# Graph attention kernel, edge stage: VectorE builds the two one-hot matrices of a chunk in four pieces each

## The reference

```python
def gt_layer(x, ntype, etype, src, dst, Wk, Wq, Wv, Wa, Watt, Wmsg, pri, skip, g, b):
    k = typed_linear(x, ntype, Wk).reshape(n, H, HS)        # q, v likewise; H = 8, HS = 16
    kT = jnp.einsum('nhd,htdo->nhto', k, Watt)              # one row per node and edge type
    vT = jnp.einsum('nhd,htdo->nhto', v, Wmsg)
    kw, m = kT[src, :, etype], vT[src, :, etype]
    a = jnp.einsum('ehd,ehd->eh', kw, q[dst]) * pri[:, etype].T / SQRT_D
    att = edge_softmax(a, dst, n)                           # softmax over the edges of one destination
    hag = jax.ops.segment_sum((m * att[:, :, None]).reshape(-1, H * HS), dst, num_segments=n)
    h = jax.nn.silu(typed_linear(hag, ntype, Wa))
    alpha = jax.nn.sigmoid(skip[ntype])[:, None]
    h = h * alpha + x * (1.0 - alpha)
    return layernorm(h) * g + b
# twice, then: layernorm(x + h @ ff_w + ff_b)
```

## Time and profile before

| what | value |
|---|---|
| device time, median of three executions | 8303.22 us |
| the profiled execution: span from first to last instruction | 7619.3 us |
| the rest of the median, outside the span | 683.9 us |
| busy POOL / DVE / PE / ACT in the span | 4322.7 / 3763.8 / 4483.6 / 1445.3 us |
| granted TensorE clock, mean over the span | 0.721 |
| L903, gathers issued by POOL | 3136 issues, 3453.7 us busy |
| L951, `to_rank` on DVE | 198 of 2283 ns |
| L946, `of_rank` on DVE | 200 of 1287 ns |

### The profile page before, as it was taken

The page is one execution under the profiler, slowest core; times in us unless marked ns, Lnnn a source line. Parts: engine busy times, 40 slices in busy tenths (PEclk is TensorE's granted clock), DMA queues, the critical chain, the costliest instruction groups (busy, mean ns, idle before and its releaser), DMA issues. The chain is left out here.

```text
span 7619.3 us, 79126 instructions
## 1 busy us (share of the span) xinstructions
PE 4483.6 (59%) x18423; PEld 3236.2 (42%) x18424; DVE 3763.8 (49%) x5261; ACT 1445.3 (19%) x3714; POOL 4322.7 (57%) x4007
## 2 busy tenths in 40 slices
PE   0128999566666665654318999566666665665221
PEld 0113443555555555554203444455555555555111
DVE  1224443555555555554374444455555555554473
ACT  0013333111111111112112333111111111111111
POOL 0543222777777777775303222677777777776305
PEclk9569999666766666666559999766666666676555
DMA  3125776666666666665103777666666666666101
GB/s 68 39 45 220 297 297 281 160 178 166 177 165 176 167 171 170 170 172 122 29 19 150 297 297 296 181 168 174 169 173 168 176 166 176 169 173 159 34 0 35
DMA packets 809561, 1228.51 MB, mean 161 GB/s; under 512 B 152983, under 2 KB 623978, under 8 KB 758833
## 3 DMA queue, kind: packets, MB, share of 16 engines
q0 software_dynamic: 223248, 853.51, 33.6%
q10 hardware_dynamic: 439680, 221.74, 11.4%
q1 hardware_dynamic: 146097, 148.81, 10.9%
HBM read 574.03 MB, written 649.66 MB: 161 GB/s over the span
## 5 line engine op out<-in xcount | busy, mean ns | idle before, releaser
L903 POOL DMA_INDIRECT kv_e<-table_d,row_s x3136 | 3453.7, 1101 | 982.1 <-issue 939.1
L1033 PE MATMUL qe_ps<-q_w,of_rank 128*128 (+1 forms) x6336 | 1149.3, 340 | 634.5 <-DVE kq L966 565.9
L1067 PE MATMUL sum_ps<-pv,to_rank 128*128 128x136 f32 x6272 | 1193.2, 373 | 261.7 <-DVE pv L985 261.7
L1033 PEld LDWEIGHTS qe_ps<-q_w,of_rank 128*128 128x128 f32 x6336 | 991.3, 240 | 767.4 <-issue 710.9
L966 DVE TENSOR_TENSOR kq<-kv_e,qe_ps 128x512 f32<-128x512 f32 x784 | 537.4, 685 | 1528.8 <-DMA kv_e<-table_d,row_s 1526.7
L1067 PEld LDWEIGHTS sum_ps<-pv,to_rank 128*128 128x128 f32 x6272 | 1154.7, 277 | 318.4 <-issue 318.4
L759 POOL DMA_INDIRECT table_d<-piece,t_row x392 | 372.7, 951 | 1041.9 <-ACT piece L811 829.7
L811 DVE COPY piece<-k_ps 128x512 f32<-128x512 f32 x784 | 541.7, 691 | 808.6 <-PE k_ps L801 808.6
L801 PE MATMUL k_ps<-edge_w,kv_t 128*128 128x512 f32 x1568 | 813.9, 601 | 2.6 <-DVE edge_w L821 2.6
L801 PE MATMUL v_ps<-edge_w,kv_t 128*128 128x512 f32 x1568 | 802.4, 593 | 0.0
L1019 ACT COPY sums<-sum_ps 128x408 f32<-128x408 f32 (+1 forms) x1176 | 522.5, 461 | 943.9 <-PE sum_ps L1067 941.8
(11 more groups left out here) (269 smaller groups left out, 3352.6 us busy)
## 6 DMA issues: line engine op xcount, KB each, us to landing
part_d<-sums ACTq DMA_DIRECT2D x196, 1088.0 KB, 6.4
local_b<-local_d SPq DMA_DIRECT2D x200, 512.0 KB, 6.4
kv_e<-table_d,row_s POOLq DMA_INDIRECT x3136, 2.8
q_w<-q_d SPq DMA_DIRECT2D x200, 64.0 KB
table_d<-piece,t_row POOLq DMA_INDIRECT x392, 4.5
flag<-start_d SPq DMA_DIRECT2D x392, 8.0 KB
q_d<-zero SPq DMA_DIRECT2D x50, 64.0 KB
max_d<-ends_max ACTq DMA_DIRECT2D x196, 1.0 KB, 4.3
```

The costliest lines, as they stand in the source:

```text
L903: pool.indirect_dma_start(out=kv_e[:, b, t, :], out_offset=None, in_=table_d, in_offset=bass.IndirectOffsetOnAxis(ap=row_s[:, b, t:t + 1], ...
L1033: last = pe.matmul(qe_ps[:, t * D:(t + 1) * D], of_rank[:, b, t, :], rows, start=True, stop=True)
L1067: last = pe.matmul(sum_ps[:, n % 3, (t - t0) * REC:(t - t0 + 1) * REC], to_rank[:, b, t, :], pv[:, b, t, :], start=True, stop=True)
```

## The change

`of_rank` of a chunk is built by four `tensor_scalar` of 128x512 in place of one of 128x2048, at the same place. `to_rank` is built by four `tensor_tensor` of 128x512; two of them stand behind the reduce of q = 1 and two behind that of q = 2, where before the whole stood behind q = 2. So the wait for `s_used` comes one quarter earlier. `s_of` and `s_to` count 4 per chunk in place of 1; TensorE waits for all four in either case.

```diff
             def spread_ranks(dve, c, b, i):
                 dve.wait_ge(s_loc[b], (i + 1) * 16)
-                dve.tensor_scalar(of_rank[:, b].rearrange("p t e -> p (t e)"), local_b[:, b, :], part[:], None,
-                                  ALU.is_equal).then_inc(s_of[b], 1)
-
-            def place_edges(dve, c, b, i):
+                for q in range(4):
+                    dve.tensor_scalar(of_rank[:, b, q * QT:(q + 1) * QT, :].rearrange("p t e -> p (t e)"),
+                                      local_b[:, b, q * QT * P:(q + 1) * QT * P], part[:], None, ALU.is_equal).then_inc(s_of[b], 1)
+
+            def place_edges(dve, c, b, i, q):
                 dve.wait_ge(s_used[b], ONE + i)
-                dve.tensor_tensor(to_rank[:, b], lane[:].unsqueeze(1).broadcast_to([P, CT, P]),
-                                  local_c[:, ds(c * CT, CT)].unsqueeze(2).broadcast_to([P, CT, P]), ALU.is_equal).then_inc(s_to[b], 1)
+                dve.tensor_tensor(to_rank[:, b, q * QT:(q + 1) * QT], lane[:].unsqueeze(1).broadcast_to([P, QT, P]),
+                                  local_c[:, ds(c * CT + q * QT, QT)].unsqueeze(2).broadcast_to([P, QT, P]), ALU.is_equal
+                                  ).then_inc(s_to[b], 1)
...
-                place_edges(dve, 0, 0, 0)
+                for q in range(4):
+                    place_edges(dve, 0, 0, 0, q)
...
-                            if q == 2:
-                                place_edges(dve, c + 1, 1 - b, i + b)
+                            if q in (1, 2):
+                                place_edges(dve, c + 1, 1 - b, i + b, 2 * q - 2)
+                                place_edges(dve, c + 1, 1 - b, i + b, 2 * q - 1)
...
-                pe.wait_ge(s_of[0], 1)
+                pe.wait_ge(s_of[0], 4)
...
-                        pe.wait_ge(s_of[1 - b], i + b + 1)
+                        pe.wait_ge(s_of[1 - b], (i + b + 1) * 4)
...
-                        pe.wait_ge(s_to[b], i + 1)
+                        pe.wait_ge(s_to[b], (i + 1) * 4)
```

## The result

The changed kernel takes 8528.47 us (median of four executions, 8505.76 to 8533.27); the kernel before, run beside it, 8298.77 us. The ratio is 1.0277, with a 95% interval of 1.0236 to 1.0318: **slower by 230 us**, where 8009 us was forecast, and outside the range of 7890 to 8150.

The account below looks back on a forecast made before the run. POOL issuing gathers end to end was taken as the bound, some issues stretched by DVE instructions. Per chunk 1.0 + 0.7 - 0.2 = 1.5 us, over 196 chunks 294 us: 8303 - 294 = 8009 us, range 7890 to 8150.

Parts of the forecast that it names:

- the 683.9 us around it are taken as unchanged: Difference between the traced span of 7619.3 us and the median of 8303.22, assumed to stay outside the change.
- POOL issues gathers end to end, and nothing else holds it: Edge stage, L903: 3453.7 us busy and 982.1 idle, nearly all issue, make up the whole stage of both layers.
- The cover that the prediction gave DVE: DVE's waits for gathered rows, 7.8 us per chunk, some 5.8 left after the change, would hide its added work.
- Rival D: DVE becomes the bound, held off by running POOL issues: chunk 22.9 us, 59 us slower, 8362 us; chance 0.04.
- The two gains: Less stretching of POOL's issues per chunk: 1.0 us from to_rank in four, 0.7 us from of_rank in four.
- a loss of 0.2 us (bounds 0 and 0.42): Per chunk, pv (L985) stretching POOL's issues more once the long of_rank instruction before it is gone.
- the cost rule of a short blocker: A DVE instruction of length d meets a POOL request with chance d/1.25 and then costs d/2.
- Rival A: POOL does not get in between DVE's pieces; gains and losses sum to 0, 8303 us; chance 0.04.
- "Right" marks: Signs of success: L903's mean about 1007 ns, median 946, no issue over 2 us; edge stages about 147 us shorter each.
- DVE's added time is covered: Pieces add 0.52 us of DVE time per chunk, hidden by waits for rows; without that cover, 102 us.

Follow-up runs that it names:

- e0_before: The kernel before, unchanged, timed and profiled a second time: 8291.35 us, span 8289.5.
- e11: The changed kernel with TensorE's spread_q signalling once per chunk instead of four times, on a prompt chip: 7505.86 us, 0.9834 of the kernel before.
- e2: The kernel before with only to_rank in four pieces, all behind q = 2, without the earlier wait: 8555.75 us, 1.0312.
- e5: The kernel before with whole instructions, to_rank and its wait for s_used moved from q = 2 to q = 1: 8403.94 us, 1.0137.
- e1: The kernel before with only of_rank in four pieces, to_rank whole behind q = 2: 8356.52 us, 1.0091.
- e7: The changed kernel plus a useless 128x2048 tensor_reduce on DVE behind q = 2 of every chunk: 8559.2 us, 1.0308.
- e9: The changed kernel with POOL waiting, before the second half of a chunk's gathers, until the previous chunk's turned scores are copied: 8409.25 us, 1.0138.
- e6: The changed kernel plus a useless 128x2048 tensor_tensor of two SBUF tiles on DVE behind q = 2: 8758.49 us, 1.0554.
- e12: The kernel before with spread_q signalling once per chunk instead of four times, on a prompt chip: 7630.84 us, 1.0003.
- e13: The kernel before with 12 useless TensorE signals more per chunk, on a prompt chip: 7631.33 us, 1.0003.
- e15: The changed kernel with spread_q signalling once per chunk instead of four times, on a late chip: 8705.43 us, 1.0481 of the kernel before.
- e17: The kernel before with 12 useless TensorE signals more per chunk, on a late chip: 8285.46 us, 1.0004.
- e8: The changed kernel with one DVE signal per matrix and one wait on s_used per pair: 8521.23 us, 1.027 of the kernel before.

## Why the prediction was wrong

**The step that failed first** is the sentence that the sum starts from: "the 683.9 us around it are taken as unchanged". A span 684 us short of every time shown was not work outside the span. The edge stage in the timed executions was bound otherwise: in e0_before POOL waits 705 us for pv, where the earlier trace rows have 43, and DVE stands 525 us before L966 (450 for rows), where the earlier trace rows have 1529. "POOL issues gathers end to end, and nothing else holds it" was true of the traced execution only.

**The wait that took the gain's place.** L903's mean is 1012 ns in the changed kernel (forecast about 1007), the median 946, none over 1.85 us. That this fits is luck: POOL stands still there while L947 runs, so that no issue can be stretched by it (6 us in all), and where POOL does not stop (e11) the mean is 1068. What decides on a late chip is TensorE's signals. Sent while gathers stream, they come many us later, in most chunks of the changed kernel when POOL has stopped. The kernel before loses 650 us in the same way, mostly at its sums (see above); the change takes away the break before the turn, and the turn is late in 194 chunks in place of 61. The cover that the prediction gave DVE, 5.8 us per chunk of waiting for rows, is gone (L969 idle 15 us). Of the parts, to_rank's pieces alone cost the most (e2), the earlier wait some (e5), of_rank's pieces little (e1). Rival D has the right sign and the wrong place: it had POOL hold DVE off instruction by instruction, but DVE's busy time grew by 85 us (3839.0 against 3754.2 in e0_before; forecast 102) and could grow by 447 more for 38 (e7).

What is shown is that holding POOL back lets the signal through (e9, 8409 beside 8521 us, copy's wait 1242 for 2744 us), and that a whole two-tensor instruction put back before the turn makes fewer turns late (e6, 74 for 192 in e7). That whole instructions keep signals prompt because they break the stream fits the table above, e6's sums included. **What stays open** is why a signal has to wait for the stream at all: late signals also come through while POOL issues (in e0_before 33 of the 61 late copies start inside an issue), and 39 of its 124 turns close behind a break are late. And why one chip is late and another not, no run here can tell.

**The terms of the sum, where signals are prompt** (e11 against e12). I put each stretched issue down to the DVE instruction that ended 0.81 us before it (or 0.13, where POOL was stopped only at its end), and added up what the issues took above their median:

```
us of stretch by the instruction that caused it     to_rank  of_rank    pv   total
e12, whole instructions                                 303      164    35     500
e11, four pieces                                         74       37   272     384
change measured                                        -229     -127  +237    -116
change forecast                                        -196     -137   +39    -294
```

(The totals are L903's busy time less 3136 medians; the rest of each is under 3 us.) The two gains are right within 17%; so is the piece of of_rank, 0.486 us (forecast 0.44), four in 1.67 us (1.50). **The mis-sized term is pv's**: "a loss of 0.2 us (bounds 0 and 0.42)" per chunk measured 237/196 = 1.2 us. I had given L985 the cost rule of a short blocker, on the strength of one issue of 1.11 us in the earlier trace rows that lay inside four of them. The timelines of e11 show the other case, POOL first, then DVE:

```profile
3022.12 1.27 POOL L903 DMA_INDIRECT kv_e<-table_d,row_s  x1 [0.30 <-issue]
3023.70 2.81 POOL L903 DMA_INDIRECT kv_e<-table_d,row_s  x1 [0.30 <-issue]
3026.81 0.95 POOL L903 DMA_INDIRECT kv_e<-table_d,row_s  x1 [0.30 <-issue]
```

```profile
3021.60 1.67 DVE L947 TENSOR_SCALAR of_rank<-local_b,part 128x512 f32<-128x512 bf16 x4
3023.18 2.49 DVE L989 TENSOR_TENSOR pv<-kv_e,pv 128x512 f32<-128x512 f32 x4
```

The issue that begins at 3023.70 ends at 3026.51, 0.84 us after the last of four pv (3025.67): it was let in between none of them. Rival A, that pieces don't let POOL in, is true of this place: 190 issues are stretched by pv, by 1.43 us on average. It is not true of to_rank's pieces, which come in pairs and lost 74 us for 303. "Right" marks fail on this too: issues over 2 us remain (108 in e11, one of 2.81 us above), and L903's mean is 1068, not 1007. On a prompt chip the change, for which e11 stands, would have been 125 us faster, 7506 us for 7631; even there the gain was forecast at over twice its size.

**What held:** POOL's issue is lengthened by L951 and L946, pieces take most of that away; DVE's added time is covered on a prompt chip (L969 still idle 1332 us in e11); the clock is no part of it (0.66 in the edge stage of e0_before and of the changed kernel alike, over windows of 2000 us).

## What to carry to other kernels

Before arguing from a profile, hold its span against the time of that execution and against the median of the others: if the two differ by more than a few us, the trace shows another condition, and a sum made against it is a sum for that condition. A cost read from one pair of rows (one 1.11 us issue) is a sample of one phase; when a term's price depends on what comes just before, look for the phase in which the neighbour that the edit removes is gone. And where one engine issues gathers without a break, a chain of short cross-engine signals beside it is what the kernel may end up waiting for, so a shorter issue need not be a gain.

## What the runs showed of the hardware

- **Signals of TensorE that come late while gathers stream.** On three of five chips the copy started on average 1 to 11 us after the turn that it waits for, over 0.3 us late in 61 to 194 of 196 chunks; in the changed kernel and e2 a median 2.4 to 2.8 us after POOL's last issue ended, in e0_before and e6 mostly while POOL issued. Of 1037 turns that ended nine or more gathers behind POOL's last break 1026 were late, of 260 in a pause 5. On the other two chips the copy was never late (0.04 us on average). Only waits on TensorE's signals are late in this way: in the 142 chunks of e0_before in which POOL was issuing, ACT's signals reached DVE in 0.03 us and TensorE in 0.05, DVE's reached ACT in 0.04 us, while TensorE's for the probabilities reached ACT up to 9.55 us late. The kernel before takes about 650 us longer on the chips that show it (8280 for 7629). The traces of late executions also hold under half as many semaphore records (42,637 in e0_before for 102,766 in the first trace; most of the missing ones are of DMA). Those of `s_turn` are nearly all there in the changed kernel, 201 of 206, so they are not why its copies read "remote". Whether the missing records have to do with the lateness is open.
- **No effect of the number of signals.** Three fewer or twelve more of TensorE's per chunk moved no time on either kind of chip (e12, e13, e15 to e17, all within 0.2%), and six fewer of DVE's left the signals late (e8). The Trainium skill (VectorE: DVE Perf Modes, section on the TRN2 errata) warns that high-rate semaphore increments of one engine can deadlock another and should be spaced. No run here shows a deadlock, and making them fewer did not help against the lateness.
- **Which instructions stop an issue.** A 128x2048 tensor_tensor of two SBUF tiles lengthens L904's busy time by 3330.8 - 3183.9 = 147 us against a tensor_reduce of the same length (e6, e7). The Trainium skill (GPSIMD Engine Reference, section 1, Specifications) says that GpSimd's SBUF interfaces are shared with VectorE and contended by instructions with two SBUF inputs or in a two-port mode; by that rule, the trace agrees for these two. of_rank has one SBUF input and stretches issues too (164 us in e12), and whether it runs in such a mode no run here shows.
- **Queued pieces let POOL in at some times only.** to_rank's pairs mostly did (290 issues stretched by 0.26 us on average in e11); the four pv behind of_rank's pieces mostly did not (190 by 1.43 us).
